# A third PSUM bank for the maximum's scores, the cross attention's product in slot 12, and the second norm behind it

## The chip, the core and the metric

The kernel runs on one core of a Trainium2 chip. The metric is the device time of one execution in microseconds; of several runs the median counts. Engines: PE is TensorE (PEld its weight loads), DVE is VectorE, ACT is ScalarE, POOL is GpSimd, SP issues most DMAs. Each engine takes its own instructions in the order of the program, and semaphores tie the engines together.

## What is computed

One decoder layer on 32 batches of 256 rows of 256 numbers:

```python
x = _layernorm(x + attn(x, Wq, Wk, Wv))          # 16 heads for q, one shared head of 16 for k and v
x = _layernorm(x + xattn(x, ctx, ctx, mask, W1, b1, W2, b2))   # one head, 120 context rows per batch
x = _layernorm(x + ffn(x, Wg, W1, b1, Wo, bo))   # 8 experts, the best 2 of each row, gated linear unit
```

The self attention is `softmax(q k^T / 4) v` per head. The cross attention sends both sides through the same two linear maps, adds a mask to the scores, and multiplies the softmax with the raw context. The last layer's gate is a softmax over 8 experts whose two largest are kept and scaled to a sum of one.

## The kernel before

`attention` is the first stage, `experts` the second; the change touches only the first. It is a software pipeline written out by hand. `pipeline` calls every engine's `step(t)` for t = 0 to 38. In step t batch t is projected (L547, L593, L596), batch t-1 is scored once for the maximum of each row (L625, reduced by DVE at L853), batch t-2 has its maxima split and transposed (L569), batch t-3 is scored a second time, exponentiated and multiplied with the values (L635, ACT L755, value product L523), batch t-4 gets its heads back in order and its first norm's statistics (L512, L811, L817, L795, L801), batch t-5 goes through the first norm and the cross attention (L677, L539, L555, L885, L723, L588, L604, L961), batch t-6 through the second norm and the gate (L795, L801, L677, L563, L577, L894 to L984), and batch t-7 is sent to the lists of its experts (L391). Steps 0 to 6 fill the pipeline, steps 32 to 38 drain it.

A step has 16 slots, `for u in range(UNITS)`. In each slot PE scores two heads for the maximum (one unit), and one more unit for the exponentials; all other work is hung on slots by `if u == ...`. The order within a slot is that of the code: on PE the special work of a slot stands ahead of the slot's scores, and a value product `pv` behind them (slots 5, 9, 13, and slot 1 of the next step ahead of its scores). On DVE the slot's reduction L853 comes first, the special work behind it. After slot 15 DVE does the tail of the gate: L973 to L984, whose last line adds the counts of the experts and raises `slot_link`.

PSUM has 8 banks of 512 f32 for each partition. Before: `psS` (2) for the maximum's scores, `psT` (2) for the others, `psO` (2) for the value products of heads 0 to 7 and 8 to 15 (g = 0, 1), `psA` and `psB` (1 each) for everything else. psA and psB are used by six things in turn. The tables `bank_a` and `bank_b` list these uses and the semaphore that tells that each was read; `bank_read` makes a use wait for the read of the one before it. For `q_projected` (L547, slot 2) that is `counted`: `slot_link` of batch t-7, which DVE raises at L984 in the tail of step t-1.

```python
bank_b = {"q_projected": ("q_rest", 0, 1, 1), "x2_transposed": ("x2t_copied", 6, 1, 1),
          "gate_scored": ("gate_link", 6, 7, 1), "cprob_transposed": ("cprobt_copied", 5, 1, 1),
          "kv_projected": ("k_rest", 0, 1, 1), "counted": ("slot_link", 6, 3, 1)}
```

Semaphores that the steps below name: `max_reduced` counts reductions, `att_copied` the copies of psO by ACT (L684), `k_split` the last third of the keys (DVE L949), which the next step's slot 0 waits for, `x1_ready` and `x2_ready` the norms by ACT (L677), whose scale and shift POOL makes from DVE's moments (L801) in four small operations (L382 to L387).

## Time and profile before

| What | us |
|---|---|
| median of 3 runs | 1473.22 (1471.83 to 1475.22) |
| the profiled execution | 1475.48 |
| its span on the core | 1472.9 |
| PE busy | 1276.2 (87%) |
| PE weight loads busy | 899.1 (61%) |
| DVE busy | 1136.1 (77%) |
| ACT busy | 755.9 (51%) |
| POOL busy | 656.9 (45%) |

The attention stage fills the span up to about 843 us, then come the tables and the weights of the experts, their tiles from about 890 to 1305, and the final sums. A row of the timeline is start, duration, engine, line, operation, output<-input, shapes and count, and in brackets the idle time before it with what ended it. A row that holds several instructions gives the time from the first one's start to the last one's end. Starts of matmuls are measured, their ends are modelled; matmuls that follow each other overlap.

### The profile page before, as it was taken

Reading aid. Unit: us, or ns where it says so; the run is one execution under the profiler, and the core shown is the slowest. Engines: PE = TensorE matmul, PEld = TensorE weight load, DVE = VectorE, ACT = ScalarE, POOL = GpSimd, SP = SyncE. Lnnn points to the kernel's source line nnn. Section 1 sums busy time; section 2 is a strip of 40 time slices with the busy share of each in tenths; the row PEclk is TensorE's granted clock in tenths of the full one; section 3 lists DMA queues with packets and bytes.
Section 4 is the critical chain, followed back from the end, with each engine's and each line's share of the span. In section 5 each row is a group of like instructions: output and inputs, shape, how many; then the busy total and the mean of one; then the engine's idle time right before and its main releaser. Section 6 shows DMA issues by size and latency. Waiting matters only on the chain. (4 is left out here: it accounts for less than half of the span.)

```text
span 1472.9 us, 29966 instructions
## 1 busy us (share of the span) xinstructions
PE 1276.2 (87%) x7668; PEld 899.1 (61%) x7669; DVE 1136.1 (77%) x3110; ACT 755.9 (51%) x1743; POOL 656.9 (45%) x1018
## 2 busy tenths in 40 slices
PE   6888999999999999999987307999999999968886
PEld 4443555555555555555544206888888888858876
DVE  1455788888888888888864387888888888859998
ACT  1125677777777777777775242223223322314444
POOL 1011244454544444545444472343334333447886
PEclk9998999999999999999997558999999999989999
DMA  4436456656646656655636522334433443369995
GB/s 101 106 61 101 80 104 132 127 117 133 122 120 128 128 116 122 129 120 117 122 107 234 197 81 84 130 130 133 137 131 130 133 137 130 130 247 322 336 334 198
DMA packets 171822, 211.67 MB, mean 144 GB/s; under 512 B 20048, under 2 KB 143056, under 8 KB 167632
## 3 DMA queue, kind: packets, MB, share of 16 engines
q1 hardware_dynamic: 147808, 143.92, 40.9%
q0 software_dynamic: 17680, 55.28, 10.1%
q10 hardware_dynamic: 6240, 11.34, 2.2%
q8 instruction: 44, 0.72, 0.2%
q14 instruction: 50, 0.41, 0.1%
HBM read 124.81 MB, written 84.89 MB: 142 GB/s over the span
## 5 line engine op out<-in xcount | busy, mean ns | idle before, releaser
L853 DVE TENSOR_REDUCE negmax<-psS 128x2 f32<-128x512 f32 x512 | 349.2, 686 | 100.1 <-PE psS L625 94.4
L755 ACT ACTIVATE probs<-psT 128x512 f32<-128x512 f32 x512 | 303.4, 598 | 171.7 <-PE psT L635 165.1
L1331 ACT ACTIVATE sig<-hb 128x512 f32<-128x512 f32 x136 | 86.1, 633 | 286.9 <-DVE hb L1414 279.8
L625 PE MATMUL psS<-kstack,qstack 96*128 96x256 bf16 x1024 | 195.4, 273 | 33.8 <-DVE kstack L949 15.3
L635 PE MATMUL psT<-qstack,kstack 99*128 99x512 bf16 x512 | 194.9, 382 | 5.1 <-ACT probs L755 5.1
L1211 POOL DMA_INDIRECT g_rows<-g,slot x136 | 135.6, 997 | 70.7 <-issue 67.4
L625 PEld LDWEIGHTS psS<-kstack,qstack 96*128 96x128 bf16 x1024 | 92.4, 104 | 90.7 <-DVE negmax L853 34.8
L391 POOL DMA_INDIRECT lists<-x,slots x128 | 127.0, 992 | 34.2 <-issue 30.3
L523 PE MATMUL psO<-probs,vaug 128*32 128x512 f32 x1024 | 140.4, 621 | 0.9 <-ACT probs L755 0.8
L1425 DVE SCALAR_TENSOR_TENSOR g<-g,xe,sig 128x512 f32<-128x512 f32 x136 | 102.2, 751 | 28.5 <-DVE g L1421 16.8
L1414 DVE TENSOR_TENSOR hb<-psHb,f_b 128x512 f32<-128x512 f32 x136 | 94.0, 691 | 37.5 <-issue 34.7
L1252 PE MATMUL psHb<-w_hi,xet_hi 128*128 x272 | 119.0, 437 | 0.0
L1206 POOL TENSOR_TENSOR away<-xe,expf 128x1 f32<-128x1 f32 x136 | 28.5, 210 | 195.1 <-DVE g L1425 188.3
L419 POOL TENSOR_TENSOR y<-att,xres 128x512 f32<-128x512 f32 x32 | 40.3, 1260 | 163.7 <-DVE att L817 163.7
L1252 PE MATMUL psHa<-w_hi,xet_hi 128*128 x272 | 107.8, 396 | 0.0
L1253 PE MATMUL psHb<-w_lo,xet_hi 128*128 x272 | 107.5, 395 | 0.0
L1253 PE MATMUL psHa<-w_lo,xet_hi 128*128 x272 | 107.2, 394 | 0.0
L404 POOL TENSOR_TENSOR qpart<-qrest,one_c 128x512 bf16<-128x512 f32 x32 | 33.3, 1040 | 158.0 <-DVE qrest L878 158.0
L1421 DVE TENSOR_TENSOR g<-psHa,f_b 128x512 f32<-128x512 f32 x136 | 93.4, 687 | 9.0 <-PE psHa L1256 6.9
L1272 PE MATMUL psX<-ident,xe 128*128 128x128 f32 x272 | 52.2, 274 | 54.7 <-DVE w_lo L1126 54.4
L1222 POOL TENSOR_TENSOR row_sum<-rows 128x512 f32<-128x512 f32 x64 | 86.6, 1377 | 9.5 <-DMA rows<-g_rows 8.2
L1256 PE MATMUL psHb<-w_hi,xet_lo 128*128 x272 | 86.2, 399 | 0.0
(201 smaller groups left out, 2950.7 us busy)
## 6 DMA issues: line engine op xcount, KB each, us to landing
rows<-g_rows SPq DMA_DIRECT2D x32, 1024.0 KB, 8.0
qstack<-q_parts SPq DMA_DIRECT2D x192, 128.0 KB
xe<-lists SPq DMA_DIRECT2D x136, 133.0 KB, 2.1
q_parts<-qpart SPq DMA_DIRECT2D x32, 384.0 KB, 2.8
sums<-x SPq DMA_DIRECT2D x32, 264.0 KB, 2.3
x2in<-sums SPq DMA_DIRECT2D x32, 264.0 KB, 4.7
xt<-in_x_t SPq DMA_DIRECT2D x32, 256.0 KB, 6.0
xres<-in_x SPq DMA_DIRECT2D x32, 256.0 KB, 3.2
```

The lines of the kernel that those rows point to most:

```text
L391: pool.indirect_dma_start(out=dram["lists"], out_offset=bass.IndirectOffsetOnAxis(ap=slots[:, b.s2, 2 * c + k:2 * c + k + 1], axis=0), in_ ...
L523: last = mm(psO[32 * i:32 * i + 32, g, :], vaug[:, b.s4, kc, :], probs[:, (4 * w + i) % PT, :], start=kc == 0, stop=kc == 1)
L625: last = mm(psS[:, u % 2, hh * S:(hh + 1) * S], qstack[0:KROWS, b1.s4, 2 * hp + hh, c * P:(c + 1) * P], kstack[0:KROWS, b1.s4, :], start=T ...
L635: mm(psT[:, u % 2, :], kstack[0:KROWS + MROWS, b3.s4, kc * P:(kc + 1) * P], heads, start=True, stop=True).then_inc(sm["scored"], 1)
L755: nc.scalar.activation(probs[:, u % PT, :], psT[:, u % 2, :], ACT.Exp, scale=SELF_SCALE).then_inc(sm["exp_done"], 1)
L853: v.tensor_reduce(negmax[:, b1.s2, 2 * hp:2 * hp + 2, c], psS[:, u % 2, :].rearrange("p (h k) -> p h k", h=2), AX.X, ALU.max, negate=True) ...
L1211: pool.indirect_dma_start(out=dram["g_rows"], out_offset=bass.IndirectOffsetOnAxis(ap=slot[:, o.s4:o.s4 + 1], axis=0), in_=g[:, o.s4], in_ ...
L1252: mm(out, hi[:, part], w_hi[:, k, columns], start=k == 0, stop=False)
L1253: mm(out, hi[:, part], w_lo[:, k, columns], start=False, stop=False)
L1414: v.tensor_tensor(hb[:, i.s2], psHb[:, i.s2, :], b1[:, bass.ds(e * H2 + H, H)], ALU.add).then_inc(sm["hb_ready"], 1)
L1421: v.tensor_tensor(g[:, i.s4], psHa[:, i.s2, :], b1[:, bass.ds(e * H2, H)], ALU.add).then_inc(sm["ha_ready"], 1)
L1425: v.scalar_tensor_tensor(g[:, i.s4], g[:, i.s4], xe[:, i.s4, bass.ds(e + D, 1)], sig[:, i.s2], ALU.mult, ALU.mult).then_inc(sm["g_ready"], 1)
```

## The change

The scores of the maximum get three banks, used in turn over all batches, so that a unit waits for the reduction three units back, not two. The bank is taken from the values: one accumulator `psO` serves both halves, and the value product waits for the copy of the half before it. Work at the start that used two banks of psO now uses psO and the second bank of psT. On PE the product of the cross attention moves from slot 14 to slot 12. On DVE the reciprocal `crec` moves from slot 13 to 11, the last third of the keys from 14 to 13, the cross attention's result `y2` from 14 to 13, and the second norm's stats and moments from slots 0 and 1 of the next step to slots 14 and 15 of the same one. ACT writes the second norm in two halves, in slots 3 and 4, and PE waits for each half apart. Hunks on the folding of the weights at the start, which only rename the banks, are left out, save one as an example.

```diff
@@ -193,9 +193,10 @@
     slots = sb("slots", [P, 2, QC * 2], U32)
     base = dram["base"]
 
-    psS = ps("psS", [P, 2, 512])
+    psS = ps("psS", [P, 3, 512])
     psT = ps("psT", [P, 2, 512])
-    psO = ps("psO", [P, 2, 512])
+    psO = ps("psO", [P, 512])
+    folded = (psO, psT[:, 1])
     psA = ps("psA", [P, 512])
     psB = ps("psB", [P, 512])
 
...
@@ -475,7 +476,7 @@
                 pe.wait_ge(sm["bias_copied"], g)
             for ic in range(DC):
                 for k in range(DC):
-                    mm(psO[:, ic, 0:GROUP], gram[:, k, ic * P:(ic + 1) * P], ctx_t[:, k, g % 2, :],
+                    mm(folded[ic][:, 0:GROUP], gram[:, k, ic * P:(ic + 1) * P], ctx_t[:, k, g % 2, :],
                        start=k == 0, stop=k == DC - 1)
             for k in range(DC):
                 last = mm(psT[:, 0, 0:GROUP], uvec_all[:, k, :], ctx_t[:, k, g % 2, :], start=k == 0,
...
@@ -518,9 +519,9 @@
             g, kc = w // 2, w % 2
             wait(pe, "exp_done", UNITS * b.n + 4 * w + 4)
             if kc == 0:
-                wait(pe, "att_copied", 2 * b.n + g - 1)
+                wait(pe, "att_copied", 2 * b.n + g)
             for i in range(4):
-                last = mm(psO[32 * i:32 * i + 32, g, :], vaug[:, b.s4, kc, :], probs[:, (4 * w + i) % PT, :],
+                last = mm(psO[32 * i:32 * i + 32, :], vaug[:, b.s4, kc, :], probs[:, (4 * w + i) % PT, :],
                           start=kc == 0, stop=kc == 1)
             last.then_inc(sm["pv_done"], 1)
 
...
@@ -556,9 +557,9 @@
                                       keymap[:, k, bass.ds(b5.n * SC, SC)], start=k == 0, stop=k == DC - 1)
                     last.then_inc(sm["cross_scored"], 1)
                 if u == 5 and active(b6):
-                    wait(pe, "x2_ready", done(b6))
                     bank_read(bank_b, t, "x2_transposed")
                     for c in range(QC):
+                        wait(pe, "x2_ready", done(b6, QC, c + 1))
                         for k in range(DC):
                             last = nc.tensor.transpose(psB[:, k * S + c * P:k * S + (c + 1) * P],
                                                        x2[:, b6.s2, c, k * P:(k + 1) * P], ident[:, :])
...
@@ -596,7 +597,7 @@
                             last = mm(psB[:, S + c * DK:S + (c + 1) * DK], xt[:, t.s2, k, c * P:(c + 1) * P],
                                       wv[:, k, :], start=k == 0, stop=k == DC - 1)
                     last.then_inc(sm["kv_projected"], 1)
-                if u == 14 and active(b5):
+                if u == 12 and active(b5):
                     wait(pe, "cprobt_copied", done(b5))
                     wait(pe, f"ctxv_loaded{b5.s2}", 16 * b5.half + 16)
                     bank_read(bank_a, t, "cross_out")
...
@@ -619,10 +620,10 @@
                     if u == 0:
                         wait(pe, f"q_stacked{b1.s2}", 6 * 16 * (b1.half + 1))
                         wait(pe, "k_split", done(b1))
-                    wait(pe, "max_reduced", UNITS * b1.n + u - 1)
+                    wait(pe, "max_reduced", UNITS * b1.n + u - 2)
                     c, hp = u // 8, u % 8
                     for hh in range(2):
-                        last = mm(psS[:, u % 2, hh * S:(hh + 1) * S],
+                        last = mm(psS[:, (UNITS * b1.n + u) % 3, hh * S:(hh + 1) * S],
                                   qstack[0:KROWS, b1.s4, 2 * hp + hh, c * P:(c + 1) * P], kstack[0:KROWS, b1.s4, :],
                                   start=True, stop=True)
                     last.then_inc(sm["max_scored"], 1)
...
@@ -681,7 +682,7 @@
         def copy_att(b, g):
             wait(act, "pv_done", 4 * b.n + 2 * g + 2)
             wait(act, "att_transposed", 2 * b.n + g - 1)
-            copy(att_t[:, g, :], psO[:, g, :]).then_inc(sm["att_copied"], 1)
+            copy(att_t[:, g, :], psO[:, :]).then_inc(sm["att_copied"], 1)
 
         def step(t):
             b2, b3, b4, b5, b6 = (t.back(k) for k in range(2, 7))
...
@@ -702,11 +703,13 @@
                     wait(act, "q_projected", done(t))
                     wait(act, "q_stored", done(t.back(2), 16))
                     copy(qpart[:, t.s2, 0].rearrange("p c s -> p (c s)"), psB[:, :]).then_inc(sm["q1_cast"], 1)
-                if u == 4 and active(b6):
+                if u == 3 and active(b6):
                     wait(act, f"x2_stored{b6.s2}", 16 * b6.half)
                     wait(act, "x2_transposed", done(b6.back(2)))
                     wait(act, f"dispatched{b6.s2}", 2 * QC * 16 * b6.half)
-                    norm(x2, rstd2, shift2, y2, b6, "rstd2_ready", "x2_ready")
+                    norm(x2, rstd2, shift2, y2, b6, "rstd2_ready", "x2_ready", range(0, 1))
+                if u == 4 and active(b6):
+                    norm(x2, rstd2, shift2, y2, b6, "rstd2_ready", "x2_ready", range(1, QC))
                 if u == 6 and active(b6):
                     wait(act, "x2_transposed", done(b6))
                     wait(act, "gate_scored", done(b6.back(2)))
...
@@ -841,8 +844,8 @@
                 for g in context_group(t, u):
                     copy_keybias(g)
 
-                if u == 1 and active(b6):
-                    wait(dve, "stats2_ready", done(b6))
+                if u == 15 and active(b5):
+                    wait(dve, "stats2_ready", done(b5))
                 if u == 9 and active(b6):
                     wait(dve, "gate_max", done(b6))
                 if u == 13 and active(b4):
...
@@ -851,18 +854,13 @@
                     wait(dve, "max_scored", UNITS * b1.n + u + 1)
                     c, hp = u // 8, u % 8
                     v.tensor_reduce(negmax[:, b1.s2, 2 * hp:2 * hp + 2, c],
-                                    psS[:, u % 2, :].rearrange("p (h k) -> p h k", h=2), AX.X, ALU.max, negate=True
+                                    psS[:, (UNITS * b1.n + u) % 3, :].rearrange("p (h k) -> p h k", h=2), AX.X, ALU.max, negate=True
                                     ).then_inc(sm["max_reduced"], 1)
-                if u == 0 and active(b6):
-                    wait(dve, "y2_ready", done(b6))
-                    stats(y2, stats2, b6, "stats2_ready")
                 if u == 0 and active(b7):
                     wait(dve, "slot_link", 3 * b7.n + 1)
                     v.tensor_tensor(chosen[:, b7.s2], hot[:, b7.s2],
                                     place[:, b7.s2].unsqueeze(2).to_broadcast([P, QC, 2, E]), ALU.mult
                                     ).then_inc(sm["slot_link"], 1)
-                if u == 1 and active(b6):
-                    moments(stats2, mv2, b6, "var2_ready")
                 if u == 1 and active(b7):
                     wait(dve, "slot_link", 3 * b7.n + 2)
                     v.tensor_reduce(slotf[:, b7.s2], chosen[:, b7.s2], AX.X, ALU.add).then_inc(sm["slot_link"], 1)
...
@@ -944,23 +942,28 @@
                     gate(5)
                     v.tensor_tensor(gden[:, b6.s2], gden[:, b6.s2], gtop[:, b6.s2, :, 1], ALU.add
                                     ).then_inc(sm["gate_link"], 1)
-                if u == 14 and active(t):
+                if u == 13 and active(t):
                     wait(dve, "k_mid", done(t))
                     v.tensor_tensor(kstack[64:80, t.s4], krest[64:80, t.s2], ksmall[64:80, t.s2], ALU.subtract
                                     ).then_inc(sm["k_split"], 1)
-                if u == 13 and active(b5):
+                if u == 11 and active(b5):
                     wait(dve, "cross_exp", done(b5))
                     v.reciprocal(crec[:, b5.s2], csum[:, b5.s2]).then_inc(sm["crec_ready"], 1)
                 if u == 14 and active(b6):
                     gate(6)
                     v.reciprocal(gden[:, b6.s2], gden[:, b6.s2]).then_inc(sm["gate_link"], 1)
-                if u == 14 and active(b5):
+                if u == 13 and active(b5):
                     wait(dve, "crec_ready", done(b5))
                     wait(dve, "cross_out", done(b5))
                     for c in range(QC):
                         last = v.scalar_tensor_tensor(y2[:, b5.s2, c, :], psA[:, c * D:(c + 1) * D],
                                                       crec[:, b5.s2, c:c + 1], x1[:, b5.s2, c, :], ALU.mult, ALU.add)
                     last.then_inc(sm["y2_ready"], 1)
+                if u == 14 and active(b5):
+                    wait(dve, "y2_ready", done(b5))
+                    stats(y2, stats2, b5, "stats2_ready")
+                if u == 15 and active(b5):
+                    moments(stats2, mv2, b5, "var2_ready")
             if t.fixed and t.n == 0:
                 copy_vectors()
             for g in context_group(t, UNITS):
```

## Rows read from the trace of the kernel before

**Rows 1.** Busy time by engine of one step: us, busy us and count; PEclk, DMA, GB/s.
```profile
409.32:431.14 21.82, 20.32 (x147) 12.68 (x145) 18.62 (x64) 16.71 (x41) 10.59 (x16) 1.00 0.56 123
```

**Rows 2.** Waits, 230 to 710 us: who <- for whom: us, times, longest.
```profile
PEld psS L625 <- DVE negmax L853: 11.3, 22, 0.5
...
DVE negmax L853 <- PE psS L625: 56.0, 110, 0.6
```

**Rows 3.** Timeline of PE and its weight loads, slot 12 to slot 2.
```profile
424.22 0.38 PE L625 MATMUL psS<-kstack,qstack 96*128 96x256 bf16 x2
...
424.95 0.39 PE L625 MATMUL psS<-kstack,qstack 96*128 96x256 bf16 x2
...
426.49 1.13 PE L604 MATMUL psA<-ctxv,cprob_t 120*128 120x256 f32 x4
427.45 0.38 PE L625 MATMUL psS<-kstack,qstack 96*128 96x256 bf16 x2
...
428.24 0.38 PE L635 MATMUL psT<-qstack,kstack 99*128 99x512 bf16 x1
429.11 0.38 PE L625 MATMUL psS<-kstack,qstack 96*128 96x256 bf16 x2 [0.49 <-DVE kstack L949]
...
430.64 0.66 PE L539 MATMUL psA<-ident,x 128*128 128x128 f32 x4
...
431.35 1.70 PEld L547 LDWEIGHTS psB<-xt,wq 128*128 128x128 f32 x8
...
431.57 1.89 PE L547 MATMUL psB<-xt,wq 128*128 128x256 f32 x8
...
433.30 0.38 PE L625 MATMUL psS<-kstack,qstack 96*128 96x256 bf16 x2
```

**Rows 4.** Timeline of DVE, slot 11 to slot 1 of the next step.
```profile
424.20 0.69 DVE L853 TENSOR_REDUCE negmax<-psS 128x2 f32<-128x512 f32 x1 [0.63 <-PE psS L625]
...
425.88 0.42 DVE L931 TENSOR_TENSOR krest<-psB,kstack 96x256 f32<-96x256 f32 x1 [0.30 <-ACT kstack L745]
...
426.99 0.69 DVE L853 TENSOR_REDUCE negmax<-psS 128x2 f32<-128x512 f32 x1
427.60 0.24 DVE L801 BATCH_NORM_AGGREGATE mv<-stats 128x2 f32<-128x6 f32 x2
...
428.60 0.42 DVE L949 TENSOR_TENSOR kstack<-krest,ksmall 16x256 bf16<-16x256 f32 x1
...
430.99 0.15 DVE L984 TENSOR_TENSOR base<-psB,base 128x8 f32<-128x8 f32 x1
...
431.66 0.74 DVE L795 BATCH_NORM_STATS2 stats<-y 128x6 f32<-128x256 f32 x2
...
433.05 0.24 DVE L801 BATCH_NORM_AGGREGATE mv<-stats 128x2 f32<-128x6 f32 x2
```

**Rows 5.** Timeline of ACT: the value copy of slot 11, the first norm.
```profile
424.92 0.58 ACT L684 COPY att_t<-psO 128x512 f32<-128x512 f32 x1
...
429.45 1.09 ACT L677 ACTIVATE x<-y,shift,rstd 128x256 f32<-128x256 f32 x2 [0.20 <-POOL shift L387]
```

**Rows 6.** Timeline around the second norm: ACT, then PE.
```profile
413.56 1.10 ACT L677 ACTIVATE x<-y,shift,rstd 128x256 f32<-128x256 f32 x2
...
414.71 0.66 PE L563 MATMUL psB<-ident,x 128*128 128x128 f32 x4 [0.88 <-ACT x L677]
415.20 0.38 PE L625 MATMUL psS<-kstack,qstack 96*128 96x256 bf16 x2
```

**Rows 7.** Timeline of the first step of the drain that has no scores for the maximum.
```profile
772.01 2.07 PE L604 MATMUL psA<-ctxv,cprob_t 120*128 120x256 f32 x4
...
774.39 1.09 ACT L755 ACTIVATE probs<-psT 128x512 f32<-128x512 f32 x2 [2.94 <-PE psT L635]
...
773.55 0.20 POOL L387 TENSOR_TENSOR shift<-nmean,rstd 128x2 f32<-128x2 f32 x1
...
775.37 1.09 ACT L677 ACTIVATE x<-y,shift,rstd 128x256 f32<-128x256 f32 x2
```

More of the change, by code:

```diff
@@ L447, in fold_projections @@
                 for k in range(DC):
-                    last = mm(psO[:, oc, 0:D], w2t[:, k, oc * P:(oc + 1) * P], w1[:, k, :], start=k == 0,
+                    last = mm(folded[oc][:, 0:D], w2t[:, k, oc * P:(oc + 1) * P], w1[:, k, :], start=k == 0,
                               stop=k == DC - 1)
@@ L458, in fold_projections @@
                 for k in range(DC):
-                    mm(psO[:, ic, 0:D], wc[:, k, ic * P:(ic + 1) * P], wc[:, k, :], start=k == 0, stop=k == DC - 1)
+                    mm(folded[ic][:, 0:D], wc[:, k, ic * P:(ic + 1) * P], wc[:, k, :], start=k == 0, stop=k == DC - 1)
             for ic in range(DC):
                 for k in range(DC):
-                    mm(psT[:, 1, ic:ic + 1], wc[:, k, ic * P:(ic + 1) * P], cvec[:, k:k + 1], start=k == 0,
+                    mm(psT[:, 0, DC + ic:DC + ic + 1], wc[:, k, ic * P:(ic + 1) * P], cvec[:, k:k + 1], start=k == 0,
                        stop=k == DC - 1)
@@ L656, in copy_projections @@
             for oc in range(DC):
-                last = copy(wc[:, oc, :], psO[:, oc, 0:D])
+                last = copy(wc[:, oc, :], folded[oc][:, 0:D])
             last.then_inc(sm["wc_copied"], 1)
@@ L660, in copy_projections @@
             for ic in range(DC):
-                last = copy(gram[:, ic, :], psO[:, ic, 0:D])
+                last = copy(gram[:, ic, :], folded[ic][:, 0:D])
             last.then_inc(sm["gram_copied"], 1)
@@ L671, in copy_keymap, with norm @@
                 load_context_group(act, g + 2)
-        def norm(x, rs, shift, y, b, ready, name):
+        def norm(x, rs, shift, y, b, ready, name, rows=range(QC)):
             wait(act, ready, done(b, 3))
-            for c in range(QC):
+            for c in rows:
                 last = nc.scalar.activation(x[:, b.s2, c, 0:D], y[:, b.s2, c, :], ACT.Identity,
```

4 lines of the change are left out of this document (2 added, 2 removed).

## The prediction

> **What bounds the kernel now.** I read the busy time of one stretch first, then the waits, then the timeline of each engine. The edits lie in the attention stage, where a new batch enters each step. A step lasts 480 / 22 = 21.82 us, since each wait of the step stands 22 times in 480 us [rows 2]. In one step TensorE is busy 20.32 us at full clock, VectorE 18.62, ScalarE 16.71 [rows 1]. So TensorE leads with 1.50 us of holes, and VectorE is 1.7 us behind it: an edit pays if it closes a hole of TensorE without making VectorE late where TensorE waits for it.
>
> Three holes recur each step. (a) The scores of slot 13 wait for a reduction, 11.3 us of weight loads in 22 steps [rows 2]. The matmuls would have come two pitches of 0.22 behind 424.22, at 424.66, and came at 424.95: 0.29 us lost [rows 3]. (b) The scores of slot 0 wait for the key split L949, 0.49 us idle. They would have come one pitch behind 428.24, at 428.46, and came at 429.11: 0.65 us lost [rows 3]. (c) The transposes of the second norm, L563 in slot 5, wait for ScalarE's norm, 0.88 us idle [rows 6].
>
> **Third bank.** Scores now wait for the reduction three units back. Only hole (a) has a reduction as releaser, so the bank by itself is worth 0.29 us a step. Its price is a single accumulator for the values: the value product of slot 13 must wait for the copy L684 of slot 11, which runs 424.92 to 425.50 [rows 5]. With the moved product ahead of it, it comes behind 425.08 (below) and two more pairs of scores, near 426.0, half a microsecond after the copy: cost nothing. Without that cover it would cost about what the bank gave, 0.1 to 0.3 us. For the other half the copy stands in slot 2 and the product in slot 5: nothing. The folding of the weights at the start keeps its order and sizes: nothing.
>
> **Cross product to slot 12.** Its four matmuls (L604) go ahead of the scores of slot 12, not behind the value product of slot 13. TensorE's work is the same, and what L604 reads is there: the bank's last read (L817) and the copy L730 belong to slot 10. Eight matmuls of this width take 431.57 to 433.30, 0.216 us each [rows 3]; four take 0.86, so the scores of slot 12 come at 424.22 + 0.86 = 425.08 and last 0.38, to 425.46. VectorE was ready for them at the end of reduction 11, 424.20 + 0.69 = 424.89 [rows 4]. Now reduction 12 starts at 425.46. An operation follows a reduction after 0.61 us (426.99 to 427.60) [rows 4], so the key rest L931 starts at 426.07 instead of 425.88, and all that follows on VectorE is 0.19 us late: the first norm's moments, reduction 13 (427.18 for 426.99).
>
> **Second norm behind it.** VectorE now does the cross result L961 before reduction 14, the second norm's stats before reduction 15 and its moments behind it, all ahead of the step's tail (L973 to L984). Stats and moments used to stand behind the tail, in slots 0 and 1. Stats cost 0.74, as reduction 15 waits for their end; moments 0.24 less the 0.08 by which an operation overlaps the next (426.99 + 0.69 against 427.60), 0.16; the reciprocal L953, gone to slot 11, gives back one short operation, some 0.08 [rows 4]. From reduction 13 to the end of L984 it took 426.99 to 431.14, 4.15 us; now 4.15 + 0.74 + 0.16 - 0.08 = 4.97, so L984 ends at 427.18 + 4.97 = 432.15.
>
> Who waits for L984? The query projection L547 in slot 2 writes bank B, whose last content is the expert count, and the table bank_b makes it wait for slot_link, which L984 raises. In the trace L984 ends at 431.14 and L547's first weight load stands at 431.35 [rows 3, 4]: the wait shows nowhere, because it just fits by 0.21 us. With 432.15 it binds. The matmul comes 0.09 behind the release (L949 ends at 429.02, scores at 429.11 [rows 3, 4]), at 432.24, and a restarted row of matmuls costs 0.10 more (four L604 took 0.96 from 426.49 to 427.45, pitches give 0.86 [rows 3]). Against 431.57 that is **0.77 us lost a step**. All of slots 2 to 11 stands behind the projection on TensorE's queue, and ScalarE's copy L704 and the second norm behind that. VectorE is late only up to slot 1; its reduction 2 waits for scores again.
>
> **Key split one slot earlier.** L949 now stands before L961 and reduction 14, about 0.9 us behind reduction 13, near 428.1, and ends near 428.5, before the 429.02 of now. But what (a) and (b) give is lost at the next wait: L539 waits for the first norm (moments 427.60, POOL's four operations, L677). L677 ends at 429.45 + 1.09 = 430.54 and L539 starts at 430.64 [rows 3, 5], no slack. With the moments 0.19 late L539 comes at 430.83. L547 waits beyond that, so this 0.19 is inside the 0.77.
>
> **Second norm in halves, slots 3 and 4.** ScalarE has no hole in front of the norm: the half moved ahead of slot 3's exponential only changes the order, so the second half is ready when both were, at 414.66, and POOL's part, now early, was not last. Two of four transposes are done before it: four took 0.49 us (414.71 to 415.20), of which two 0.11 pitches go, **0.22 us gained a step** [rows 6]. Bounds: 0, if both halves still go together, and 0.49, if all were ahead; I take the middle, which is the program's order.
>
> **Sum.** L547 stands behind such a tail in steps 7 to 31, 25 times: 25 x (0.77 - 0.22) = +13.8 us. In the drain no projections are left, VectorE is idle, and the moved product helps: in two steps ScalarE's exponential waits 2.9 us because L604 stands ahead of slot 14's scores for 1.9 us [rows 7]. POOL's shift is ready at 773.75 and L677 starts at 775.37, so at most 1.5 us comes free, 3.0 in two steps. In the last batch the stats go ahead of the tail, an estimated 0.65 (six short operations at some 0.1 each), and the split gives 0.22. Together -3.9. The later stages are untouched. The profiled execution took 1475.48 us, 2.3 above the median 1473.22, its span 1472.9. 1475.5 + 13.8 - 3.9 = 1485.4, less 2.3: **1483** for the median.
>
> **Rivals.** (1) *TensorE is short of banks.* If it can run ahead with three banks so that VectorE is never late (it decides at L984 ending before about 431.3), holes (a) and (b) and the split all come in: 0.29 + 0.65 + 0.22 = 1.16 a step, 25 x 1.16 + 3.9 = 33 us: 1440. For it: VectorE waits 56.0 us in 22 steps for scores [rows 2], time for the 0.9 us of norm. Against it: from reduction 12 to L984 its queue has a single hole, the 0.30 at L931 [rows 4], and the moved work stands there. The Trainium skill (Perfetto Trace Analysis, Optimization Strategy) says that one gap repeating on the engine that should be saturated can mean too little PSUM; by that rule up to the whole 1.50 us a step could go, while the trace puts a bank behind one hole of three. (2) *L547 does not bind, L539 does.* If VectorE regains 0.8 us ahead of L984, the late moments (+0.19) and the split (-0.22) cancel and the drain remains: 1469. It decides at L984 ending by about 431.5. (3) *Costs without gains.* The queue of VectorE is 0.1 us longer than summed, the split and the drain give nothing: 25 x 0.87 = +22: 1495. (4) *It does not do what it says*: bank and order move nothing on balance, drain gains meet small losses, 1471 to 1476.
>
> **How the numbers follow.** Forecast 0.58, own range 1477 to 1490 (stall of 0.6 to 0.9, drain -2 to -5); rival 1 0.13, rival 2 0.14, rival 3 0.09, rival 4 0.06. From 1466 to 1492 leaves out rival 1 and most of rival 3, 2 in 10. About 0.2% (3 us) is what a measurement of this kernel can tell from no change. Faster: rival 1 and most of 2, 0.25; same: rival 4 and the edges of 2 and the forecast, 0.12; slower 0.63.
>
> **What would show it.** Steps of about 22.37 us for 21.82; a new wait of L547 for L984 with about 0.6 us of idle TensorE; no scores waiting for reductions; L539 waiting for L677, 0.2 us or more; L563 in two pairs; the 2.9 us waits of the drain shorter by over 1 us. It is wrong if L984 ends before L547's turn, or if the moved norm fits into VectorE's waits.

## The result: slower by 0.4%, as forecast in sign, and the profile after

The changed kernel takes 1478.17 us (median of 20 runs, 1473.94 to 1482.26), the kernel before 1472.16 in the same comparison (20 runs, 1462.82 to 1478.84). The ratio is 1.0044, 95% interval 1.0028 to 1.0059: +6 us, where +9.8 was forecast. The profiled execution took 1478.79 us with a span of 1476.1, against 1475.48 and 1472.9.

One step of the pipeline after, the answer to [rows 1] (us, then busy time and count of PE, PEld, DVE, ACT and POOL, granted clock, DMA share, GB/s):

```profile
410.28:432.77 22.49, 20.76 (x145) 12.68 (x144) 18.62 (x65) 16.63 (x41) 10.89 (x17) 1.00 0.60 120
```

VectorE is busy exactly as long as it was, 18.62 us, and the clock is full. The step is longer by 22.486 - 21.822 = 0.66 us (each is the time from the start of the query projection of step 8 to that of step 31, divided by 23). Forecast was 0.77 - 0.22 = 0.55. The waits of 230 to 710 us, to be read beside [rows 2] (who <- for whom: us, times, longest):

```profile
DVE negmax L856 <- PE psS L626: 76.2, 127, 0.9
PEld psA L540 <- ACT x L678: 36.6, 21, 1.8
PE psA L540 <- ACT x L678: 17.6, 21, 0.8
PE psB L548 <- DVE base L987: 4.3, 22, 0.2
```

TensorE now waits 22 times for the count read L987 (L984 before), which it did not show once before, and 21 times for the first norm in front of L540 (L539 before). VectorE itself waits more for scores, 76.2 us for 56.0: it is not short of time, it is late at one place. Timeline of TensorE, slot 11 to slot 5, beside [rows 3] and [rows 6]:

```profile
424.70 0.38 PE L636 MATMUL psT<-qstack,kstack 99*128 99x512 bf16 x1
424.92 1.03 PE L605 MATMUL psA<-ctxv,cprob_t 120*128 120x256 f32 x4
425.78 0.38 PE L626 MATMUL psS<-kstack,qstack 96*128 96x256 bf16 x2
...
426.75 1.07 PE L524 MATMUL psO<-probs,vaug 128*32 128x512 f32 x8
...
429.35 0.38 PE L626 MATMUL psS<-kstack,qstack 96*128 96x256 bf16 x2 [0.22 <-DMA qstack<-q_parts]
...
431.78 0.66 PE L540 MATMUL psA<-ident,x 128*128 128x128 f32 x4 [0.84 <-ACT x L678]
432.28 0.38 PE L626 MATMUL psS<-kstack,qstack 96*128 96x256 bf16 x2
432.50 0.38 PE L636 MATMUL psT<-qstack,kstack 99*128 99x512 bf16 x1
433.07 1.97 PE L548 MATMUL psB<-xt,wq 128*128 128x256 f32 x8 [0.19 <-DVE base L987]
434.87 0.38 PE L626 MATMUL psS<-kstack,qstack 96*128 96x256 bf16 x2
...
437.49 0.44 PE L564 MATMUL psB<-ident,x 128*128 128x128 f32 x2 [0.26 <-DVE qrest L876]
438.11 0.44 PE L564 MATMUL psB<-ident,x 128*128 128x128 f32 x2 [0.18 <-ACT x L678]
438.38 0.38 PE L626 MATMUL psS<-kstack,qstack 96*128 96x256 bf16 x2
```

To compare steps I count from the start of slot 11's second scores: 424.00 before (one pitch of 0.22 ahead of slot 12's scores at 424.22), 424.70 after. Slot 12's scores came at 0.22 and come at 1.08, as forecast. Slot 0's scores come at 4.65, no longer at 5.11; they still follow the key split, by 0.10 us (L947 ends at 429.25). But L540 comes at 7.08 where it was 6.64, L548 at 8.37 where it was 7.57, and slot 2's scores at 10.17 where they were 9.30. That is 0.87 lost. From there to slot 5's scores it is 3.51 us; before, it took 3.72 (from 433.30 - 21.82 = 411.48 to the scores at 415.20 of [rows 6]). That is 0.21 won. 0.87 - 0.21 = 0.66: the whole of the step's difference. VectorE's and GpSimd's side of it, beside [rows 4] and [rows 5]:

```profile
427.91 0.69 DVE L856 TENSOR_REDUCE negmax<-psS 128x2 f32<-128x512 f32 x1
428.52 0.24 DVE L804 BATCH_NORM_AGGREGATE mv<-stats 128x2 f32<-128x6 f32 x2
...
428.83 0.42 DVE L947 TENSOR_TENSOR kstack<-krest,ksmall 16x256 bf16<-16x256 f32 x1
429.28 0.88 DVE L959 SCALAR_TENSOR_TENSOR y<-psA,crec,x 128x256 f32<-128x256 f32 x2
...
430.74 0.73 DVE L798 BATCH_NORM_STATS2 stats<-y 128x6 f32<-128x256 f32 x2
431.51 0.69 DVE L856 TENSOR_REDUCE negmax<-psS 128x2 f32<-128x512 f32 x1
...
432.77 0.15 DVE L987 TENSOR_TENSOR base<-psB,base 128x8 f32<-128x8 f32 x1
```

```profile
428.84 0.46 POOL L383 TENSOR_TENSOR vare<-mv,eps_c 128x2 f32<-128x2 f32 x1 [0.92 <-DVE mv L804]
...
430.64 1.09 ACT L678 ACTIVATE x<-y,shift,rstd 128x256 f32<-128x256 f32 x2 [0.87 <-POOL shift L388]
```

The statistics of the second norm (L798, 0.73) stand in front of the last reduction, and L987 ends at 432.92, 8.22 behind the reference, where it ended at 7.14. And GpSimd's first operation on the moments takes 0.46 us. Before it took 0.19:

```profile
427.92 0.19 POOL L382 TENSOR_TENSOR vare<-mv,eps_c 128x2 f32<-128x2 f32 x1 [0.68 <-DVE mv L801]
```

**Where the total comes from.** Two profiles of each kernel were taken (the second of each is an experiment below). Fill is the start of the query projection of step 7; steady, from there to that of step 31; drain, from there to the last count read:

| kernel | step | fill | steady | drain | span |
|---|---|---|---|---|---|
| before | 21.822 | 191.36 | 523.90 | 122.06 | 1472.87 |
| before, again | 21.822 | 189.96 | 523.90 | 119.35 | 1467.99 |
| after | 22.486 | 185.62 | 539.77 | 115.55 | 1476.1 |
| after, again | 22.527 | 183.94 | 540.72 | 114.30 | 1474.73 |

"Drain" ends at the start of the last count read. By the means of each two: fill -5.9, steady +16.3, drain -5.8, the sum +4.6 of +5.0 in the spans. The steady part repeats within 1 us, fill and drain within 1.3 to 2.7.

### The profile page after: what moved, and what is told of

Read it like the earlier page. It is cut to its first block and busy times, and to the rows that moved or that the text cites. A ratio compares the mean times of both kernels' runs of the same rounds, so it can differ in the third digit from the quotient of the medians.

```text
span 1476.1 us, 29968 instructions
## 1 busy us (share of the span) xinstructions
PE 1277.3 (87%) x7668; PEld 897.3 (61%) x7669; DVE 1137.6 (77%) x3110; ACT 753.6 (51%) x1743; POOL 665.4 (45%) x1018
## 5 line engine op out<-in xcount | busy, mean ns | idle before, releaser
L636 PE MATMUL psT<-qstack,kstack 99*128 99x512 bf16 x512 | 195.2, 383 | 4.6 <-ACT probs L758 3.3
L524 PE MATMUL psO<-probs,vaug 128*32 128x512 f32 x1024 | 137.2, 608 | 1.6 <-ACT probs L758 0.8
L678 ACT ACTIVATE x<-y,shift,rstd 128x256 f32<-128x256 f32 x128 | 73.5, 600 | 38.4 <-POOL shift L388 37.6
```

The source lines that it names most:

```text
L524: last = mm(psO[32 * i:32 * i + 32, :], vaug[:, b.s4, kc, :], probs[:, (4 * w + i) % PT, :], start=kc == 0, stop=kc == 1)
L636: mm(psT[:, u % 2, :], kstack[0:KROWS + MROWS, b3.s4, kc * P:(kc + 1) * P], heads, start=True, stop=True).then_inc(sm["scored"], 1)
```

## Experiments

### Statistics of the second norm back behind the tail

The changed kernel with `stats` and `moments` of the second norm in slots 0 and 1 of the next step again:

```diff
-                if u == 14 and active(b5):
-                    wait(dve, "y2_ready", done(b5))
-                    stats(y2, stats2, b5, "stats2_ready")
-                if u == 15 and active(b5):
-                    moments(stats2, mv2, b5, "var2_ready")
+                if u == 0 and active(b6):
+                    wait(dve, "y2_ready", done(b6))
+                    stats(y2, stats2, b6, "stats2_ready")
+                if u == 1 and active(b6):
+                    moments(stats2, mv2, b6, "var2_ready")
```

> The changed kernel with one thing undone: the second norm's stats and moments on VectorE stand behind the step's tail again (slots 0 and 1), all else as changed. Theory (the count's read L984 gates the query projection, the first norm gates behind it): the projection's wait for the count goes, the steady step falls from 22.48 to 22.04 us (21.82 + 0.44 for the late first norm - 0.22 for the halves). Rival A (the late first norm is the whole cost, the projection's wait is hidden behind it): step stays within 0.1 of 22.48. Rival B (the moved stats are the whole cost): step of 21.6, 21.82 less the halves' 0.22.

Step 22.100 (22.04 expected), median 1469.67 us against 1470.95, ratio 1.0000 (0.9977 to 1.0023). The wait for the count read is gone from the list, the one for the first norm stays as it was:

```profile
PEld psA L540 <- ACT x L678: 36.8, 21, 1.8
```

So 0.39 us a step hangs on where the statistics stand, and the rest of the loss, 22.10 - 21.82, on something that this edit leaves: the late first norm. In this trace L540 comes at 7.09, 0.45 later than in the kernel before, slot 2's scores at 9.75 for 9.30, and the halves give back 0.2 by slot 5.

### The count read at the head of the tail

The changed kernel, with everything left in its slot but `place` and `base` (L986, L987) moved ahead of L976:

```diff
             if active(b6):
+                wait(dve, "counted", done(b6))
...
+                v.tensor_tensor(then, count[:, QC, :], now, ALU.add).then_inc(sm["slot_link"], 1)
                 gate(7)
...
-                v.tensor_tensor(then, count[:, QC, :], now, ALU.add).then_inc(sm["slot_link"], 1)
```

> The changed kernel with the two count operations (place and base) moved to the head of VectorE's tail, ahead of the four small ones; nothing else. Theory: the last read of the count ends about 0.5 us earlier, the projection waits 0.1 us or less beyond the first norm, step 22.05 to 22.12 us for 22.48. Rival (VectorE's total work gates, not this read): step stays at 22.48, since VectorE does the same work.

Step 22.104, one run at 1465.0. VectorE has all its work ahead of the tail as in the changed kernel, only the operation that TensorE waits for stands ahead of four small ones. The count read ends at 7.80 instead of 8.22, and the step is that of the first experiment. It is the moment of the count read that costs, not VectorE's load.

### The third bank alone

The kernel before with the bank edits only (psS with 3 banks, one psO, the waits changed with them):

```diff
-                    wait(pe, "max_reduced", UNITS * b1.n + u - 1)
+                    wait(pe, "max_reduced", UNITS * b1.n + u - 2)
...
-                wait(pe, "att_copied", 2 * b.n + g - 1)
+                wait(pe, "att_copied", 2 * b.n + g)
```

> The kernel before with the third score bank and the single value accumulator alone. Theory: the wait of the scores of slot 13 goes, but the value product of slot 13 waits for its accumulator's copy instead, and the key split and first norm stand where they stood; step 21.82 us, within 0.05. Rival (TensorE is short of banks, the step's holes are the reductions'): step 21.5 us or less.

Step 21.968, one run at 1470.73: the bank alone costs 0.15. Its price shows in front of slot 13's value product:

```profile
422.56 0.38 PE L626 MATMUL psS<-kstack,qstack 96*128 96x256 bf16 x2
422.97 0.39 PE L636 MATMUL psT<-qstack,kstack 99*128 99x512 bf16 x1
423.54 1.06 PE L524 MATMUL psO<-probs,vaug 128*32 128x512 f32 x8 [0.18 <-issue]
```

Slot 13's scores come one pitch behind slot 12's, the wait for the reduction is gone as promised. The value product stands 0.98 behind them, where the changed kernel has 0.53 (426.22 to 426.75): the second scores (L636) come 0.19 late, and the product idles another 0.18, which this row puts down to nothing, but the waits of the same trace put down to ScalarE's copy (L685) 20 times. It starts 1.64 behind slot 11's second scores (421.90), where it was 1.49. The prediction's "without that cover 0.1 to 0.3 us" was right, the expectation written for this run (21.82) was not.

### The cross product in slot 12 alone

The kernel before with L604's block moved:

```diff
-                if u == 14 and active(b5):
+                if u == 12 and active(b5):
                     wait(pe, "cprobt_copied", done(b5))
```

> The kernel before with the cross attention's product alone moved from slot 14 to slot 12 on TensorE. Theory: reductions 12 and 13 and the first norm's moments come 0.2 us late, and all behind them: step 22.0 to 22.05 us for 21.82; POOL's first small operation of the first norm takes its usual 0.19 us, since the key split is still behind reduction 14 on VectorE. Rival (the product fills the hole of slot 13): step 21.5 us, 0.29 less.

Step 22.028, +0.21 as expected, one run at 1468.73. The delay of reduction 12 reaches L539 (6.84 for 6.64) by two ways that end together, and this run does not tell them apart: through the moments the first norm starts 0.23 late, and through the key split slot 0's scores come at 5.32 for 5.11. GpSimd's operation on the moments takes 0.19 us here.

### The kernels before and after again

Both unchanged, for how far fill and drain repeat.

> The kernel before, unchanged, once more, for its fill and its drain. Theory: the steady step of 21.82 us repeats to 0.01, and the fill (to the projection of step 7, 191.4 us in the profile of before, 184 to 188 in the five others) is one draw of several, since TensorE's granted clock falls there at other moments in each execution: this one falls between 183 and 192. Rival: the changed kernels have a shorter fill by what they do, and this one repeats 191 within 1 us.

> The changed kernel, unchanged, once more, for its fill and its drain. Theory: step 22.48 us again to 0.01; the fill to step 7 (185.6) moves by some us either way, and the drain from the last projection to the last count (115.6, for 122.1 in before) repeats within 2 us, since its order is what changed. Rival: the drain is a draw too and comes back near 122.

The results are in the table above: the steps repeat to 0.00 and 0.04 us (0.01 was expected of both), fill to 1.4 and 1.7, drain to 2.7 and 1.3. The single runs took 1470.64 and 1477.35 us.

### The norm's halves alone

```diff
-                    wait(pe, "x2_ready", done(b6))
...
+                        wait(pe, "x2_ready", done(b6, QC, c + 1))
...
-                    norm(x2, rstd2, shift2, y2, b6, "rstd2_ready", "x2_ready")
+                    norm(x2, rstd2, shift2, y2, b6, "rstd2_ready", "x2_ready", range(0, 1))
+                if u == 4 and active(b6):
+                    norm(x2, rstd2, shift2, y2, b6, "rstd2_ready", "x2_ready", range(1, QC))
```

> The kernel before with the second norm in two halves alone (ScalarE slots 3 and 4, TensorE waiting for each half apart). Theory: two transposes go ahead of the last wait, step 21.60 us (21.82 - 0.22), the whole about 5.5 us faster. Rival A: both halves become ready together behind something else, step 21.82. Rival B: the first half comes before POOL has its scale and shift in slot 3, ScalarE waits, and the step is longer than 21.82.

Step 21.651 (-0.17), fill 184.07, drain 116.10. Median 1460.94 us against 1472.35, ratio 0.9919 (0.9890 to 0.9947). This one edit of the change is worth more alone than with the rest. The steps explain 24 x 0.17 = 4.1 us of it; the remainder sits in fill and drain. As the second norm first runs in step 6, this edit can hardly be what makes its fill 6 to 7 us shorter than those of the kernel before.

### Three moves: halves, key split in slot 13, first norm's transposes in slot 2

```diff
-                if u == 14 and active(t):
+                if u == 13 and active(t):
                     wait(dve, "k_mid", done(t))
...
-                if u == 1 and active(b5):
+                if u == 2 and active(b5):
                     wait(pe, "x1_ready", done(b5))
```

> The kernel before with three small moves and no third bank: the second norm in halves; the last third of the keys on VectorE in slot 13, ahead of reduction 14; the first norm's transposes on TensorE at the head of slot 2, behind the scores of slot 1, where they have 0.44 us of slack. Theory: the key split's wait falls by up to 0.65 and the first norm takes it up only beyond 0.44; 0.22 for the halves; step 21.2 to 21.4 us, the whole 10 to 15 us faster. Rival A: the key split now meets POOL's first small operation (0.46 us for 0.19, as in the changed kernel), the norm is 0.27 late and eats most of it: step 21.4 to 21.6. Rival B: VectorE becomes the bound, no gain beyond the halves' 0.22.

Step 21.804, where 21.2 to 21.4 was expected: all that the halves gave is lost again. Median 1469.57 against 1472.35, ratio 0.9981 (0.9960 to 1.0001). The trace names the reason. First DVE, then PE:

```profile
428.31 0.42 DVE L951 TENSOR_TENSOR kstack<-krest,ksmall 16x256 bf16<-16x256 f32 x1
...
428.85 0.67 DVE L855 TENSOR_REDUCE negmax<-psS 128x2 f32<-128x512 f32 x1
```

```profile
429.66 0.38 PE L625 MATMUL psS<-kstack,qstack 96*128 96x256 bf16 x2 [0.64 <-DVE negmax L855]
```

The key split is early now, but it pushed reduction 14 back, and slot 0's scores need that reduction's bank. With two banks one wait is swapped for another: slot 0 comes 5.26 behind slot 11's second scores (424.40), where it was 5.11. In 5 of the 22 steps these scores wait up to 1.1 us for the DMA that stacks the queries instead. Most steps take 21.71 to 21.78, so a few hundredths of the mean are the DMA's.

### The same with the third bank

The three moves and the bank edits together; against the kernel with the three moves:

```diff
-    psS = ps("psS", [P, 2, 512])
+    psS = ps("psS", [P, 3, 512])
...
-    psO = ps("psO", [P, 2, 512])
+    psO = ps("psO", [P, 512])
...
-                    wait(pe, "max_reduced", UNITS * b1.n + u - 1)
+                    wait(pe, "max_reduced", UNITS * b1.n + u - 2)
```

> The kernel before with the norm's halves, the key split in slot 13 and the first norm's transposes at the head of slot 2, now with the third bank as well. Theory: with two banks the moved key split only swaps one wait for another (slot 0's scores then wait for reduction 14, step 21.80); with the third bank they wait for neither, so slot 0 comes near 4.6 us behind slot 11's second scores, where it was 5.1. The first norm is then the next in line (its scale is late by the 0.27 of GpSimd's stretched operation), so not all comes in: step 21.50 to 21.65. Rival A: the value product of slot 13, which waits for its copy (+0.15 alone), passes on through the key split: 21.75 to 21.80. Rival B: the two waits together were all that held the step: 21.3 or less.

Step 21.547, in the middle of what was expected; median 1457.54 us, ratio 0.9916 (0.9894 to 0.9939). Slot 0's scores come at 442.83, 4.60 behind slot 11's second scores, and wait for nothing:

```profile
438.23 0.38 PE L636 MATMUL psT<-qstack,kstack 99*128 99x512 bf16 x1
...
439.86 1.06 PE L524 MATMUL psO<-probs,vaug 128*32 128x512 f32 x8 [0.18 <-ACT att_t L685]
...
442.83 0.38 PE L626 MATMUL psS<-kstack,qstack 96*128 96x256 bf16 x2
```

The bank is worth 21.804 - 21.547 = 0.26 us a step beside the moved key split (0.2 against the steps in which no DMA came in between), and -0.15 without it.

### The key split behind the cross attention's result

The changed kernel, with L947 moved behind L959, both still in slot 13: it takes the key split away from the moment at which GpSimd works on the moments.

```diff
-                if u == 13 and active(t):
-                    wait(dve, "k_mid", done(t))
-                    v.tensor_tensor(kstack[64:80, t.s4], krest[64:80, t.s2], ksmall[64:80, t.s2], ALU.subtract
-                                    ).then_inc(sm["k_split"], 1)
...
                     last.then_inc(sm["y2_ready"], 1)
+                if u == 13 and active(t):
+                    wait(dve, "k_mid", done(t))
+                    v.tensor_tensor(kstack[64:80, t.s4], krest[64:80, t.s2], ksmall[64:80, t.s2], ALU.subtract
+                                    ).then_inc(sm["k_split"], 1)
```

> The changed kernel with the key split behind the cross attention's result, both still in slot 13, so that it does not run beside GpSimd's first operation on the first norm's moments. Theory of the collision: that operation takes 0.19 us again instead of 0.46, and the first norm's transposes come 0.25 us earlier against slot 11 (6.83 behind its second scores, not 7.08). Slot 0's scores come some 0.8 us later, which the 0.84 us of idle TensorE in front of those transposes just about holds. Since the count read at the tail's end, which is not moved, sets the query projection: step 22.45 to 22.55, as in the changed kernel. Rival: the 0.46 is a matter of the operation's place behind a long rest of GpSimd and stays, transposes at 7.08. Rival 2: the key split's late end costs the step 0.1 us or more.

GpSimd's operation is short again:

```profile
432.50 0.19 POOL L383 TENSOR_TENSOR vare<-mv,eps_c 128x2 f32<-128x2 f32 x1 [0.92 <-DVE mv L804]
```

and ScalarE's norm starts at 434.02, 5.67 behind slot 11's second scores (428.35), where it was 5.94: the 0.27 is back, so the collision is shown. The rest of the expectation failed, and rival 2 of it holds: the step is 22.727, 0.24 longer, one run at 1486.93. L540 starts straight behind a value product, at 6.97, since slot 0's scores came only at 5.44, and the count read ends at 8.36 (436.71), 0.14 later than in the changed kernel:

```profile
433.79 0.38 PE L626 MATMUL psS<-kstack,qstack 96*128 96x256 bf16 x2 [1.01 <-issue]
...
435.32 0.66 PE L540 MATMUL psA<-ident,x 128*128 128x128 f32 x4
...
436.86 1.97 PE L548 MATMUL psB<-xt,wq 128*128 128x256 f32 x8 [0.45 <-DVE base L987]
```

L548 comes at 8.51 here and at 8.37 in the changed kernel: 0.14 of the 0.24. Most of the rest sits in slot 10, where the transposes L513 follow the value product ahead of them by 1.11 us instead of 0.99. They write bank A, and VectorE's read of it (L820) ends only 0.15 ahead of them, where it ended 0.43 ahead in the changed kernel.

### Both norms in halves

The kernel with the second norm's halves, with the first norm treated alike:

```diff
-                    wait(pe, "x1_ready", done(b5))
...
+                        wait(pe, "x1_ready", done(b5, QC, c + 1))
...
-                    norm(x1, rstd1, shift1, y1, b5, "rstd1_ready", "x1_ready")
+                    norm(x1, rstd1, shift1, y1, b5, "rstd1_ready", "x1_ready", range(0, 1))
+                    norm(x1, rstd1, shift1, y1, b5, "rstd1_ready", "x1_ready", range(1, QC))
```

> The kernel with the second norm's halves alone (step 21.65), with the first norm written and waited for in halves as well. Theory: the transposes stand there right behind a value product, and of the wait for the norm only some 0.1 us is left to win: step 21.50 to 21.60, 1 to 4 us less than the halves alone. Rival: a second restart of TensorE between the pairs costs what the earlier start gives: 21.65 to 21.70. Rival 2: 0.22 again, as in the second norm: 21.45 or less.

Step 21.715 against 21.651, median 1462.59 us, ratio 0.9953 (0.9931 to 0.9974): nothing gained, 0.06 lost. That is near the number of the first rival, but not by its cause: the four L539 start together behind the value product (421.88 behind 420.88), with no second restart. The 0.06 sits in slot 10, where L512 follows the value product by 1.11 instead of 1.05. A wait is only worth splitting where TensorE idles in front of it; here a value product fills the time.

### Both halves in slot 3

The kernel with the three moves and the bank, the second half moved ahead of slot 3's exponential as well:

```diff
-                if u == 4 and active(b6):
+                if u == 3 and active(b6):
                     norm(x2, rstd2, shift2, y2, b6, "rstd2_ready", "x2_ready", range(1, QC))
```

> The kernel with the three moves and the bank (step 21.55), with both halves of the second norm in slot 3, one behind the other, ahead of slot 3's exponential. Theory: the first transposes wait there for VectorE's read of bank B (0.26 us idle), not for the norm, and only the second pair waits for ScalarE (0.33 us), whose half stands behind an exponential. With both halves ahead of the exponential this wait goes: step 21.20 to 21.35. Rival: the exponential, now 0.5 us later, delays the value product of slot 5 by as much as is won: 21.45 to 21.60. Rival 2: the bank's read and the restart of the pairs set the time, nothing moves: 21.55.

Step 21.084, median 1443.62 us (4 runs, 1440.94 to 1448.55), ratio 0.9833 (0.9790 to 0.9875): the best of all, and shorter than the expected 21.20 to 21.35. First the kernel with the halves apart, then this one:

```profile
428.39 0.44 PE L564 MATMUL psB<-ident,x 128*128 128x128 f32 x2 [0.26 <-DVE qrest L881]
429.15 0.44 PE L564 MATMUL psB<-ident,x 128*128 128x128 f32 x2 [0.33 <-ACT x L678]
429.43 0.38 PE L626 MATMUL psS<-kstack,qstack 96*128 96x256 bf16 x2
```

```profile
439.83 0.73 PE L564 MATMUL psB<-ident,x 128*128 128x128 f32 x4 [0.26 <-DVE qrest L881]
440.39 0.38 PE L626 MATMUL psS<-kstack,qstack 96*128 96x256 bf16 x2
```

From the first transpose to the next scores it is 0.56 us for 1.04: 0.48 less, of which 0.33 is the wait that was counted on and the rest the second restart, which was not. The step fell by 0.46. TensorE's first pair waits for VectorE's read of bank B either way, so the norm had only to be ready by then. (TensorE still waits for each half apart here; only the moment of the second half differs.) In this kernel the earlier slot for the whole norm is worth more than the halves.

## Why the prediction held, and where it did not

- **The stall of the projection**: right in place and cause. L987 ends 1.08 later than L984 did, and the projection waits for it in all 22 steps; the first two experiments take the wait away in two ways and land on the same step. Its size was 0.87, not 0.77: the count read ends 0.07 later than the sum had it (8.22 for 8.15), the projection's matmul follows 0.15 behind its end instead of 0.09, and the restart costs 0.07 instead of 0.10.
- **The cross product**: right in size. Reduction 12 starts at 1.50 (forecast 1.46), reduction 13 at 3.21 (3.18), and alone the move costs 0.21 a step (0.19).
- **The first norm**: mis-sized. "L539 comes at 430.83" is 0.19 behind its old place; it came 0.44 behind. The missing 0.25 is GpSimd's first operation, which runs beside the moved key split and takes 0.46 us for 0.19. Here it was hidden, as the projection waited longer still. It sets what remains once the stall is taken away: 0.44 - 0.21 = 0.23 of the 0.28 us by which the first experiment's step is longer than that of before. Moving an operation on one engine lengthened one on another; the sum had no term for that.
- **The second norm's halves**: right in size: 0.21 in the changed kernel, 0.17 alone, 0.22 forecast. The sum had only the norm in front of the first pair; it is VectorE's read of bank B (0.26 idle for L876) that sets its start now.
- **The bank**: "only hole (a) has a reduction as releaser, so the bank by itself is worth 0.29 us" counted waits as they stood and not as they would stand. Alone it costs 0.15, beside an earlier key split it gives 0.26, since it is then slot 0's scores that need it. In the changed kernel it does what it is for (slot 0 comes at 4.65), but all of that is lost at L540 and L548. The cover of the value copy held: the product of slot 13 waits for nothing.
- **The drain**: right in sign; how it is made up is not shown. The two waits of 2.9 us of [rows 7] are gone, the longest of ScalarE for scores behind 768 us is 0.94, and the last two count reads lie 8.53 apart where it was 10.41, 1.9 us less for the last batch, where 0.87 was summed. The answer to the first row of [rows 7], one wait of 0.94 for one of 2.94:

```profile
777.46 0.60 ACT L758 ACTIVATE probs<-psT 128x512 f32<-128x512 f32 x1 [0.94 <-PE psT L636]
```

  But the waits of 2.9 us were not the product's alone. The four matmuls of L604 take 2.07 us in [rows 7] and 1.13 in [rows 3]: from 770.7 to 774.1 the granted clock is 0.50, the lower level, and again from 791.1 to 794.5, at the second of the two waits. The second profile of the kernel before has the same place at full clock, and there the wait is 1.30:

```profile
770.00 1.13 PE L604 MATMUL psA<-ctxv,cprob_t 120*128 120x256 f32 x4
...
771.38 1.08 ACT L755 ACTIVATE probs<-psT 128x512 f32<-128x512 f32 x2 [1.30 <-issue]
```

  Nor is the -5.8 shown to come from the moved product. The drain is 117.5 with that move alone, and 116.1 with the halves alone, which leave the product in its place. With -5.8 for -3.9 the term was small by 1.9, within the spread of the two profiles of before (2.7).
- **The fill**: missing from the sum. It is 5.9 us shorter by the means, 5.7 in the first profiles. Of these, 3.9 lie between the first two projections (34.80 us before, 30.88 after), where TensorE starts slow and speeds up at other moments. The same eight matmuls of the folding, before and then after:

```profile
23.64 3.41 PE L459 MATMUL psO<-wc 128*128 128x256 f32 x8 [0.32 <-DVE cvec L776]
```

```profile
23.41 1.13 PE L460 MATMUL psO<-wc 128*128 128x256 f32 x4 [0.32 <-DVE cvec L779]
24.38 1.03 PE L460 MATMUL psT<-wc 128*128 128x256 f32 x4
```

  This part follows no edit. The kernel with the cross product alone moved, an edit that first acts in step 5, has 30.89 there as well, and the second profile of the changed kernel 32.28. Over the 14 profiles it lies between 30.89 and 37.48 with the folding in its old banks and between 30.88 and 36.74 with it in the new ones. Behind that, both kernels lose time to the lower clock at different projections. From the third to the fourth, and from there to the fifth (the first projection counted as 0; first before, then after, columns as above):

```profile
103.43:124.50 21.07, 17.53 (x102) 7.68 (x101) 12.86 (x25) 11.40 (x24) 2.19 (x2) 0.94 0.53 89
124.50:147.72 23.22, 20.31 (x115) 10.09 (x114) 14.72 (x32) 12.76 (x26) 5.34 (x8) 0.87 0.49 80
```

```profile
98.74:121.41 22.67, 18.87 (x102) 8.98 (x101) 12.88 (x25) 11.17 (x23) 2.19 (x2) 0.88 0.49 83
121.41:141.98 20.57, 17.55 (x115) 9.38 (x114) 14.58 (x32) 12.63 (x26) 5.57 (x8) 1.00 0.56 90
```

  In the second of the two stretches the same 115 matmul records take 20.31 us at a granted clock of 0.87 of the full 2.4 GHz and 17.55 at full clock, and it is 2.65 us shorter; in the first the changed kernel has the lower clock, and is 1.60 longer. In the kernel before, the clock falls to the lower level at 142.6 us, while TensorE waits 1.44 us for the DMA that stacks the queries, and is back at full at 149.4. The second profile of before repeats this dip (22.58 us at 0.89), and none of the other kernels has one between 130 and 190 us, though the changed kernel waits 1.48 us at that place too. So it may go with that kernel's schedule. What brings it on stays open: over the 14 profiles the fill lies between 181.8 and 192.4 us, 184.1 with the halves alone and 192.4 with the three moves, in no order that the edits explain. I changed nothing in the fill on its own.
- **The sum**: +16.3 steady, over 24 steps, for 13.8 forecast over 25; -5.8 drain for -3.9; -5.9 fill for 0. The sign is the stall's. That the total lies 5 us from the forecast, and not further, is in part luck, as two missed gains and one mis-sized loss partly cancelled: with the stall as measured (25 x 0.10) and nothing else changed, the forecast would have been 2.5 us above the one given, and further from the result.
- **The rivals**: in rival 1 the mechanism was real but needed another order of the work: with bank, early key split, later transposes and the norm in slot 3, and without the statistics ahead of the tail, the step is 21.08. In the change itself only the halves' 0.21 of its 1.16 us a step was kept; in the last experiment 21.82 - 21.08 = 0.74 was, 0.46 of it by the norm in slot 3, which rival 1 did not have. Rival 2's condition, a count read that no longer binds, is met in the first two experiments, and their step is 22.10, not its 21.8: it had the norm 0.19 late, and it was 0.44. The Trainium skill's rule on one gap repeating on the busiest engine (Perfetto Trace Analysis, Optimization Strategy), which can point to too little PSUM, is not borne out by the bank alone (+0.15) and is borne out for slot 0 once the key split is early (-0.26).

## What to carry to other kernels

Before moving work ahead of a step's tail, look up every operation in the tail that another engine waits for without any wait showing: one that just fits, by 0.21 us here, is as hard a limit as one that shows. A buffer is worth what the schedule around it can use: price it together with the moves that need it, not from the waits that stand in the trace of before. And where a consumer waits for something else first, have the producer's whole work done by then rather than splitting it. Before taking a long wait in the trace as the price of the work in front of it, compare the length of that work with its length elsewhere: here over half of 2.94 us was gone at full clock.

## What the runs showed of the hardware that was not expected

A small GpSimd operation is stretched by one of VectorE at the same time. `vare<-mv,eps_c`, 128x2 f32, took 0.46 us in each of the 151 cases between 230 and 710 us (seven profiles of six kernels) in which VectorE's subtraction L947 (16x256, both inputs and the output in SBUF) ran at its start, and 0.19 to 0.26 us in every other. The operation behind it started 0.42 later (428.84 to 429.26), where it was 0.15 before, so it is no artefact of how ends are recorded. In the rows of the result, L947 ends at 429.25 and GpSimd's operation at 429.30. The Trainium skill (SBUF — State Buffer, Who interferes with whom) says that a VectorE instruction with two inputs in SBUF contends with a GpSimd instruction that reads SBUF, through a shared read interface, and that the shared ports are an exclusive lock. The trace agrees that the later one waits until the first is done, 0.05 us between the two ends.

The same happens the other way round, and it stood in the trace of before. A small VectorE subtraction whose inputs and output lie in SBUF takes 0.18 us (L834 of the changed kernel, 128x32, nothing of GpSimd beside it), and another of the same size 0.65 where it starts beside a long GpSimd operation, which it outlasts by 0.05:

```profile
414.12 1.04 POOL L404 TENSOR_TENSOR qpart<-qrest,one_c 128x512 bf16<-128x512 f32 x1 [1.18 <-DVE qrest L878]
414.55 0.65 DVE L835 TENSOR_TENSOR mpart<-mrest,mpart 128x32 bf16<-128x32 f32 x1
```

It took 0.65 us in all 309 cases between 230 and 710 us of the 14 profiles, each beside that operation. Overlap alone is not enough, though: in the kernel before, the key split L949 starts in all 22 steps beside GpSimd's `rstd` (L385, 0.72 us, begun earlier) and takes 0.42 as elsewhere, so the rule as quoted says too much for that pair. With that limit, these rows and the rule gave reason to price the early key split before the run.

Four f32 transposes that start together reach the next scores in 0.56 us; as two pairs with a wait of 0.33 between them they take 1.04, so the second start costs 0.15 beside the wait. In the changed kernel it is 0.89 with a wait of 0.18, 0.15 again; against the 0.49 us that the four took in [rows 6] it would be 0.22.
